# Channel attention: values from split operands, another order of the first units, and a normalisation in fours

## The chip, the cores and the metric

The kernel runs on one core of a Trainium2 chip. The metric is the device time of one execution in microseconds (us). The core has TensorE (PE in the profile, with its weight loads as PEld), VectorE (DVE), ScalarE (ACT), GpSimd (POOL) and SyncE (SP), which here issues the transfers. The engines run side by side and wait for each other through semaphores.

## The reference, cut to what matters

Four layers follow each other: a cross attention over few keys, the channel attention of this change, a transformer block with two attentions and a feed-forward part, and a recurrent block. The change is in the second one, cut here to its core:

```python
for i in range(2):
    s, e = (bounds[i], bounds[i + 1])
    h = jnp.einsum('od,bdl->bol', Wq_list[i], z1ss[:, :, s:e])
    h = h + jnp.einsum('od,bdl->bol', Wi_list[i], u1ss[:, :, s:e])
    chunks.append(h)
q, k, v = jnp.split(jnp.concatenate(chunks, axis=2), 3, axis=1)
...
score = jnp.einsum('bndi,bndj->bnij', q + r_w_bias, k) * SCALE
prob = jax.nn.softmax(score, axis=-1)
attn_vec = jnp.einsum('bnij,bndj->bndi', prob, v)
x = jnp.einsum('od,bdl->bol', Wo, attn_vec) + bo + z1ss
return (x - mean) * jax.lax.rsqrt(var + LN_EPS)
```

There are 8 batch rows of 256 channels and 512 positions, 16 heads of 64, and the mean and variance run over the channels.

## The kernel before, in words

The stage works in 64 units: 8 passes over pairs of heads, and in each pass 8 batch rows. Seven passes are a loop, the eighth is written out. The inputs of a batch row, `zu` (128 partitions, four slots, 512 columns), hold both sources.

Queries and keys are three products of split operands: a number is rounded to a short float32 form (`hi`, type fp32r) and the rest is rounded to the same form (`lo`); the sum of hi x lo, lo x hi and hi x hi stands for the full product. ScalarE rounds the inputs and the weights, GpSimd subtracts to split the inputs (`x_lo`, line 775), VectorE does so for the weights (`w_lo`, line 811). In a projection the weights are stationary and 256 columns of inputs stream, 24 products for queries and 24 for keys.

Values come out turned, positions on the partitions. There the inputs are stationary (a block of 128x128) and 128 columns of the weights `wv` stream; both are plain float32, which the trace shows as two passes a product, each with its own load (line 547).

Within unit b TensorE does, in this order: scores 0 and 1 of the next unit, the transposes of strip 2, queries of the unit after next, the transposes of strip 3, keys of the unit after next, the mix of probabilities and values, scores 2 and 3 and transposes 0 of the next unit, values of the unit after next, transposes 1 of the next unit, and the output product. The two halves of a transposed strip are copied by ScalarE (line 695) and VectorE (line 828), and a strip's transposes wait for the copies of the strip before. Maxima are VectorE's, exponentials ScalarE's, and GpSimd scales the probabilities (line 780).

The order on each engine is written out by hand: the pieces of a prologue, then `unit`. After the last unit each batch row is normalised: TensorE means by a product with a constant matrix (line 643), VectorE subtracts (line 900), ScalarE squares, TensorE takes variances (line 651), ScalarE takes the logarithm and the exponential (lines 758 and 760), GpSimd multiplies (line 802), and SyncE stores.

Of the kernel before, what the change touches and what calls it, by code (L numbers as in the profile page):

```python
# [5 lines left out]
P = 128  # L6
# [362 lines left out]
def channel_attention(nc, semaphores, z, c, w_qk, w_v, w_o, bo, q_bias, out):  # L369
# [7 lines left out]
    SCALE = DH ** -0.5  # L377
    with ExitStack() as ctx:
# [8 lines left out]
        def sem(name, per_unit=0):  # L387
# [5 lines left out]
        w_raw = sb("w_raw", [P, 2, 2 * SLOTS, P])  # L393
        w_hi, w_lo = (sb("w_" + n, [P, 2, 2 * SLOTS, P], F32R) for n in ("hi", "lo"))
        wv = sb("wv", [P, 2 * SLOTS, P])
# [20 lines left out]
        w_loaded, wv_loaded, wo_loaded, qb_loaded, bo_loaded, acc_loaded = (  # L416
            sem(n + "_loaded") for n in ("w", "wv", "wo", "qb", "bo", "acc"))
# [10 lines left out]
        means_summed, centred, squared, vars_summed, logged, rooted, normed, stored = (  # L428
            sem(n) for n in ("means_summed", "centred", "squared", "vars_summed", "logged", "rooted", "normed", "stored"))
# [28 lines left out]
        def _(sp):  # L458
            open_loop(sp, loop_sems)

            def load_w(g):
                sp.dma_start(w_raw[:, :, :, :].rearrange("p a s o -> p (a s o)"), pair_of(w_qk, g)).then_inc(w_loaded, 16)

            def load_wv(g):
                sp.dma_start(wv[:, :, :].rearrange("p s o -> p (s o)"), pair_of(w_v, g)).then_inc(wv_loaded, 16)
# [27 lines left out]
            def unit(g, b, there):  # L493
                if there(3):
                    reload_zu(g, b + 3)
                if there(BATCH):
                    if b == 0:
                        sp.wait_ge(w_split, 2 * g)
                        load_w(g)
                    if b == 1:  # L500
                        sp.wait_ge(wo_split, 1 * g)
                        load_wo(g)
                    if b == 5:
                        sp.wait_ge(q_kept, of(g, 7, 1, 0))
                        load_qb(g)
                        sp.wait_ge(v_summed, of(g, 7, 1, 0))
                        load_wv(g)

            each_pass(sp, unit)
            for b in range(BATCH):  # L510
                sp.wait_ge(normed, b + 1)
                sp.dma_start(batch_rows(out, b), acc[:, b, :, :]).then_inc(stored, 16)
# [3 lines left out]
        def _(pe):  # L516
# [12 lines left out]
            def queries(g, b):  # L529
                pe.wait_ge(x_split, of(g, b, 1, 0))  # L530
                if b % BATCH == 0:
                    pe.wait_ge(w_split, 2 * g + 1 if b else 1)
                project(0, ps_a, b).then_inc(q_summed, 1)

            def keys(g, b):
                if b % BATCH == 0:
                    pe.wait_ge(w_split, 2 * g + 2 if b else 2)
# [108 lines left out]
            def variances(b):  # L646
                pe.wait_ge(squared, b + 1)
                if b >= 2:
                    pe.wait_ge(logged, b - 1)
                for m in range(CT):  # L650
                    mm = pe.matmul(ps_s[:, b % 2, 1, :], mean_of[:, :], pr[b % 2][:, m, :], start=(m == 0), stop=(m == CT - 1))
                mm.then_inc(vars_summed, 1)
# [8 lines left out]
        def _(act):  # L661
            def round_w(part, count):
                act.wait_ge(w_loaded, 16 * count)
# [83 lines left out]
            def squares(b):  # L747
                act.wait_ge(centred, b + 1)
                if b >= 2:
                    act.wait_ge(vars_summed, b - 1)  # L750
                act.activation(pr[b % 2][:, :, :], acc[:, b, :, :], ACT.Square).then_inc(squared, 1)

            def root(b):
                act.wait_ge(vars_summed, b + 1)
                if b >= 2:
                    act.wait_ge(normed, b - 1)
                rstd = pr[2][:, b % 2, :]
                act.activation(rstd, ps_s[:, b % 2, 1, :], ACT.Ln, bias=eps[:, 0:1]).then_inc(logged, 1)
                act.wait_ge(logged, b + 1)
                act.activation(rstd, rstd, ACT.Exp, scale=-0.5).then_inc(rooted, 1)  # L760

            for b in range(BATCH + 1):
                if b < BATCH:
                    squares(b)
                if b >= 1:
                    root(b - 1)

        @block.gpsimd
        def _(pool):
# [13 lines left out]
            split_inputs(1, 0)  # L783
# [15 lines left out]
            each_pass(pool, unit)  # L799
            for b in range(BATCH):  # L800
                pool.wait_ge(rooted, b + 1)
                pool.tensor_tensor(acc[:, b, :, :], acc[:, b, :, :], pr[2][:, b % 2, :].unsqueeze(1).to_broadcast([P, CT, FEAT]),
                                   ALU.mult).then_inc(normed, 1)

        @block.vector
        def _(dve):
            dve.memset(mean_of[:, :], 1.0 / TOK).then_inc(mean_made, 1)

            def split_w(part, count):
                dve.wait_ge(w_rounded, 2 * count + part - 1)  # L810
# [38 lines left out]

            split_w(0, 1)  # L850
            split_w(1, 1)
            keep_values(1, 0)
# [3 lines left out]
            inverse(1, 0, 1)  # L856
            tops(1, 0, 2)
# [38 lines left out]
            for b in range(BATCH):  # L896
# [4 lines left out]
                ins.then_inc(centred, 1)  # L901

# [1791 lines left out]
def build(nc, semaphores, ap, out):  # L2694
# [9 lines left out]
    channel_attention(nc, semaphores, x1, ap["c"], *(ap["L1_" + n] for n in ("w_qk", "w_v", "w_o", "bo", "q_bias")), x2)  # L2704
# [16 lines left out]
def lay_out(np, a):  # L2721

    out = {}
# [32 lines left out]
    if "L1_xattn_Wo" in a:  # L2756
# [4 lines left out]
        put("L1_w_qk", w[:, :, :2].reshape(pairs, P, -1))  # L2761
        put("L1_w_v", w[:, :, 2])
# [55 lines left out]
```

## Time and profile before

| | |
|---|---|
| median of 3 runs | 4070.14 us (4067.51 to 4077.97) |
| profiled execution | 4071.54 us, its span 4069.7 us |
| mean granted TensorE clock | 0.947 |
| busy: PE, PEld | 3572.6 us (88%), 2696.4 us (66%) |
| busy: DVE, ACT, POOL | 2260.3 us (56%), 1821.8 us (45%), 1998.3 us (49%) |

The span runs from the first to the last instruction of one execution. Busy shares are averages over stages with different limits. Matmuls overlap, so a record of one is longer than the distance to the next one.

### The profile page before, as it was taken

The page shows a single profiled execution, that of the slowest core. Times are in us where ns is not written, and L with a number is a line of the kernel's source. Part 1 is how long each engine was busy: PE and PEld are TensorE (multiplying, and loading weights), DVE is VectorE, ACT ScalarE, POOL GpSimd, SP SyncE. Part 2 cuts the span into 40 slices and gives each one's busy share as a digit, 9 for nine tenths or more (in the row PEclk, how much of TensorE's full clock was granted, in tenths as well). Part 3 has the DMA queues.
Part 4 walks back from the last instruction along what each step waited for, and adds up shares of the span by engine and source line. Part 5 has one row for each costly group of instructions (what it writes and reads, how often), then busy time and mean ns, then how long its engine had stood idle before and what let it go on. Part 6 is the DMA issues. An engine that isn't in the chain of part 4 may idle for free. (4 is left out here: it accounts for less than half of the span.)

```text
span 4069.7 us, 64007 instructions
## 1 busy us (share of the span) xinstructions
PE 3572.6 (88%) x23616; PEld 2696.4 (66%) x23616; DVE 2260.3 (56%) x2778; ACT 1821.8 (45%) x4207; POOL 1998.3 (49%) x1015
## 2 busy tenths in 40 slices
PE   8969999999999999859989997699967888888876
PEld 5757676777777677547777775588845555555543
DVE  2435454444444444447777766555427777767772
ACT  1135454555555455556666665444422332323321
POOL 1145555555555555335555554355525555555552
PEclk9989999999999999989999999799979999998988
DMA  4231111111111111020021110300030000000000
GB/s 134 67 127 58 54 58 54 68 43 58 53 59 58 54 58 53 21 96 27 26 68 48 43 39 23 106 21 21 16 129 6 12 17 17 17 7 12 12 11 16
DMA packets 107558, 189.87 MB, mean 47 GB/s; under 512 B 13344, under 2 KB 32032, under 8 KB 105632
## 3 DMA queue, kind: packets, MB, share of 16 engines
q1 hardware_dynamic: 105120, 181.97, 13.1%
q8 instruction: 191, 3.13, 0.3%
q10 hardware_dynamic: 2176, 4.19, 0.3%
q14 instruction: 71, 0.58, 0.0%
HBM read 160.97 MB, written 25.17 MB: 46 GB/s over the span
## 5 line engine op out<-in xcount | busy, mean ns | idle before, releaser
L780 POOL TENSOR_TENSOR l_pr<-l_pr,l_inv 128x1024 f32<-128x1024 f32 x256 | 485.9, 1919 | 429.7 <-DVE l_inv L824 429.7
L690 ACT ACTIVATE l_pr<-l_ps_s,l_top 128x512 f32<-128x512 f32 x512 | 348.1, 691 | 385.3 <-DVE l_top L820 385.3
L1156 POOL TENSOR_TENSOR tok_pr<-tok_pr,tok_ma 128x1024 f32<-128x1024 f32 x128 | 308.0, 2407 | 309.2 <-DVE tok_pr L1530 295.2
L2288 POOL TENSOR_TENSOR rec_rs<-rec_sE,rec_rT 128x1024 f32<-128x1024 f32 x128 | 321.8, 2515 | 248.3 <-DVE rec_sE L2675 246.2
L775 POOL TENSOR_TENSOR l_x_lo<-l_zu,l_x_hi 128x2048 fp32r<-128x2048 f32 x64 | 289.5, 4523 | 274.0 <-ACT l_x_hi L674 274.0
L820 DVE TENSOR_REDUCE l_top<-l_ps_s 128x2 f32<-128x1024 f32 x256 | 301.3, 1216 | 57.8 <-PE l_ps_s L557 57.8
L565 PEld LDWEIGHTS l_ps_t<-l_ident,l_pr 128*128 128x128 f32 x2048 | 227.8, 142 | 104.5 <-issue 103.0
L2675 DVE TENSOR_TENSOR_SCAN rec_sE<-rec_wE,rec_ps_v 128x1024 f32<-128x1024 f32 x128 | 292.7, 2286 | 4.9
L557 PE MATMUL l_ps_s<-l_k,l_q 64*128 64x512 f32 x1024 | 264.6, 637 | 29.8 <-issue 29.8
L565 PE MATMUL l_ps_t<-l_ident,l_pr 128*128 128x128 f32 x2048 | 275.3, 278 | 3.6 <-ACT l_pT L695 3.6
L1400 ACT ACTIVATE tok_pr<-tok_pr,tok_shift 128x256 f32<-128x256 f32 x512 | 253.8, 499 | 27.6 <-DVE tok_shift L1538 27.3
L836 DVE TENSOR_TENSOR l_o_lo<-l_ps_a,l_o_hi 128x512 fp32r<-128x512 f32 x64 | 44.2, 691 | 381.3 <-ACT l_o_hi L700 381.3
L547 PE MATMUL l_ps_b<-l_wv,l_zu 128*128 128x128 f32 x2048 | 239.4, 275 | 0.0
L1538 DVE TENSOR_REDUCE tok_shift<-tok_pr 128x4 f32<-128x1024 f32 x128 | 155.7, 1217 | 149.6 <-POOL tok_pr L1156 147.9
L577 PE MATMUL l_ps_a<-l_pT,l_v 128*64 128x512 f32 x1024 | 235.5, 602 | 1.8 <-ACT l_pT L695 1.8
L547 PEld LDWEIGHTS l_ps_b<-l_wv,l_zu 128*128 128x128 f32 x2048 | 234.0, 192 | 0.0
L828 DVE COPY l_pT<-l_ps_t 128x512 f32<-128x512 f32 x256 | 175.4, 685 | 70.7 <-PE l_ps_t L565 70.2
L557 PEld LDWEIGHTS l_ps_s<-l_k,l_q 64*128 64x128 f32 x1024 | 91.2, 192 | 167.8 <-issue 167.3
L695 ACT ACTIVATE l_pT<-l_ps_t 128x512 f32<-128x512 f32 x256 | 152.4, 595 | 70.4 <-PE l_ps_t L565 70.4
L524 PE MATMUL l_ps_a<-l_x_hi,l_w_lo 128*128 128x256 f32 x512 | 151.7, 296 | 32.2 <-POOL l_x_lo L775 32.2
L1240 PE MATMUL tok_ps_t<-tok_ident,tok_pr 128*128 128x128 f32 x1024 | 143.1, 285 | 32.0 <-DVE tok_pT L1543 13.0
L1787 POOL TENSOR_TENSOR mlp_cube<-mlp_cube,mlp_pre 128x512 f32<-128x512 f32 x64 | 89.6, 1400 | 163.8 <-DVE mlp_cube L1950 163.8
(357 smaller groups left out, 9385.1 us busy)
## 6 DMA issues: line engine op xcount, KB each, us to landing
l_zu<-x SPq DMA_DIRECT2D x64, 512.0 KB, 3.7
l_zu<-in_c SPq DMA_DIRECT2D x64, 512.0 KB, 4.6
l_w_raw<-in_L_w_qk SPq DMA_DIRECT2D x8, 1024.0 KB, 7.6
tok_xs<-x SPq DMA_DIRECT2D x16, 512.0 KB, 3.7
x<-tok_xb SPq DMA_DIRECT2D x16, 512.0 KB, 2.8
l_xt<-in_xT SPq DMA_DIRECT2D x8, 512.0 KB, 6.5
l_ct<-in_cT SPq DMA_DIRECT2D x8, 512.0 KB, 7.8
l_xn<-in_x SPq DMA_DIRECT2D x8, 512.0 KB, 4.7
```

What stands on the lines that cost most here:

```text
L547: mm = pe.matmul(ps_b[:, t * P:(t + 1) * P], zu[b % 2][:, s, t * P:(t + 1) * P], wv[:, t // 2 * SLOTS + s, :], start=(s == 0), stop=(s == ...
L557: pe.matmul(ps_s[:, t % 2, h, :], q[b % 2][own(h), t * P:(t + 1) * P], k[b % 2][own(h), :], start=True, stop=True).then_inc(scored, 1)
L565: mm = pe.transpose(ps_t[h][:, m, :], pr[t][:, h, m * P:(m + 1) * P], ident[:, :])
L577: mm = pe.matmul(ps_a[own(h), :], v[b % 2][:, t, own(h)], pT[h][:, t, :], start=(t == 0), stop=(t == QT - 1), skip_group_check=True)
L690: act.activation(pr[t][:, h, :], ps_s[:, t % 2, h, :], ACT.Exp, bias=top[:, t, h:h + 1], accum_out=mass[:, t, h:h + 1]).then_inc(exped, 1)
L775: pool.tensor_tensor(x_lo[b % 2][:, :, :], zu[b % 2][:, :, :], x_hi[b % 2][:, :, :].bitcast(F32), ALU.subtract).then_inc(x_split, 1)
L780: pool.tensor_tensor(pr[t][:, :, :], pr[t][:, :, :], inv[:, t, :].unsqueeze(2).to_broadcast([P, 2, FEAT]), ALU.mult).then_inc(scaled, 1)
L820: dve.tensor_reduce(top[:, t, :], ps_s[:, t % 2, :, :], AXIS.X, ALU.max, negate=True).then_inc(topped, 1)
L1156: pool.tensor_tensor(tile, tile, ma[u][:, :, :].rearrange("p t k -> p (t k)").unsqueeze(1).to_broadcast([P, 2, TT * TOK]), ALU.add).then_i ...
L1400: ins = act.activation(tile, tile, ACT.Exp, bias=shift[n % RING][:, i, m:m + 1], accum_out=mass[n // 2 % 2][:, m, n % 2 * 2 + i:n % 2 * 2 ...
L2288: pool.tensor_tensor(rs[j % 2][:, :, :], sE[j % 2][:, :, :], rT[s][:, :, :], ALU.mult).then_inc(rs_made, 1)
L2675: dve.tensor_tensor_scan(sE[j % 2][:, :, :].rearrange("p c t -> p (c t)"), wE[s][:, :, :].rearrange("p c t -> p (c t)"), ps_v[j % 2][:, :, ...
```

## The change

Values become three products of split operands: the inputs' split halves, which are there for queries and keys, are stationary, and 128 columns of split weights stream. The weights of the values join `w_raw`, `w_hi` and `w_lo` as a third part; ScalarE rounds and VectorE splits them in unit 6 of each pass but the last. Each part has its own load. Inputs are loaded again after the split of two units before, without a wait for the values, and the rounding of inputs waits for the values of two units before in place of the keys.

In the prologue the first inputs are loaded ahead of the weights, the first unit's inputs are split on VectorE, the second unit's are rounded ahead of the first queries' copy, and the first two scores stand ahead of the first values.

In the normalisation GpSimd squares (into the memory of the turned probabilities `pT`), ScalarE does four logarithms and then four exponentials, twice, and the final product is GpSimd's for four batch rows and VectorE's for four.

```diff
-        w_raw = sb("w_raw", [P, 2, 2 * SLOTS, P])
...
-        wv = sb("wv", [P, 2 * SLOTS, P])
+        w_raw = sb("w_raw", [P, 3, 2 * SLOTS, P])
...
             def reload_zu(g, b):
-                sp.wait_ge(v_summed, of(g, b - 2, 1, 0))
                 sp.wait_ge(x_split, of(g, b - 2, 1, 0))
                 load_zu(b)
 
-            load_w(0)
             load_zu(0)
-            load_wv(0)
+            load_w(0, 0)
+            load_w(0, 1)
+            load_zu(1)
+            load_w(0, 2)
             load_qb(0)
-            load_zu(1)
...
                     if b == 0:
-                        sp.wait_ge(w_split, 2 * g)
-                        load_w(g)
+                        sp.wait_ge(w_split, 3 * g)
+                        for part in range(3):
+                            load_w(g, part)
...
             def values(g, b):
-                pe.wait_ge(zu_loaded[b % 2], zu_there(g, b))
                 pe.wait_ge(k_kept, of(g, b, 1, 0))
                 if b % BATCH == 0:
-                    pe.wait_ge(wv_loaded, 16 * g + 16 if b else 16)
+                    pe.wait_ge(w_split, 3 * g + 3 if b else 3)
                 for t in range(QT):
+                    here = slice(t * P, (t + 1) * P)
                     for s in range(SLOTS):
-                        mm = pe.matmul(ps_b[:, t * P:(t + 1) * P], zu[b % 2][:, s, t * P:(t + 1) * P],
-                                       wv[:, t // 2 * SLOTS + s, :], start=(s == 0), stop=(s == SLOTS - 1), skip_group_check=True)
+                        for x, w in ((x_hi, w_lo), (x_lo, w_hi), (x_hi, w_hi)):
+                            mm = pe.matmul(ps_b[:, here], x[b % 2][:, s, here], w[:, 2, t // 2 * SLOTS + s, :],
+                                           start=(s == 0 and w is w_lo), stop=(s == SLOTS - 1 and w is w_hi and x is x_hi),
+                                           skip_group_check=True)
...
             queries(1, 1)
-            values(1, 0)
             score(1, 0, 0)
             score(1, 0, 1)
+            values(1, 0)
...
             def round_inputs(g, b):
                 act.wait_ge(zu_loaded[b % 2], zu_there(g, b))
-                act.wait_ge(k_summed, of(g, b - 2, 1, 0))
+                act.wait_ge(v_summed, of(g, b - 2, 1, 0))
...
+            round_inputs(1, 0)
             round_w(0, 1)
-            round_inputs(1, 0)
             round_w(1, 1)
+            round_inputs(1, 1)
+            round_w(2, 1)
             keep_queries(1, 0)
             keep_keys(1, 0)
-            round_inputs(1, 1)
...
                 if there(1):
                     exponentials(g, b + 1, 0)
+                if b == 6 and there(BATCH):
+                    act.wait_ge(v_summed, of(g, 7, 1, 0))
+                    round_w(2, g + 1)
                 keep_turned(g, b, 2)
...
-            def squares(b):
-                act.wait_ge(centred, b + 1)
...
+            def logarithm(b):
+                act.wait_ge(vars_summed, b + 1)
+                act.activation(pr[b // 2][:, b % 2, :], ps_s[:, b % 2, 1, :], ACT.Ln, bias=eps[:, 0:1]).then_inc(logged, 1)
...
+            for first in (0, HALF):
+                for b in range(first, first + HALF):
+                    logarithm(b)
+                for b in range(first, first + HALF):
+                    root(b)
...
-            split_inputs(1, 0)
+            pool.wait_ge(x_split, of(1, 0, 1, 0))
             split_inputs(1, 1)
...
+            def squares(b):
+                pool.wait_ge(centred, b + 1)
+                if b < 2:
+                    pool.wait_ge(mixed, of(PAIRS, BATCH - 1, 2, 1))
+                else:
+                    pool.wait_ge(vars_summed, b - 1)
+                pool.tensor_tensor(pT[b % 2][:, 0:CT, :], acc[:, b, :, :], acc[:, b, :, :], ALU.mult).then_inc(squared, 1)
+
             for b in range(BATCH):
+                squares(b)
+            for b in range(HALF):
                 pool.wait_ge(rooted, b + 1)
...
+            dve.wait_ge(x_rounded, of(1, 0, 1, 0))
+            dve.tensor_tensor(x_lo[0][:, :, :], zu[0][:, :, :], x_hi[0][:, :, :].bitcast(F32), ALU.subtract).then_inc(x_split, 1)
             split_w(0, 1)
             split_w(1, 1)
-            keep_values(1, 0)
+            split_w(2, 1)
             tops(1, 0, 0)
             tops(1, 0, 1)
             inverse(1, 0, 0)
             inverse(1, 0, 1)
+            keep_values(1, 0)
...
                     tops(g, b + 1, 1)
+                if b == 6 and there(BATCH):
+                    split_w(2, g + 1)
                 keep_turned(g, b, 2)
...
+            for b in range(HALF, BATCH):
+                dve.wait_ge(rooted, b + 1)
+                dve.tensor_tensor(acc[:, b, :, :], acc[:, b, :, :], pr[b // 2][:, b % 2, :].unsqueeze(1).to_broadcast([P, CT, FEAT]),
+                                  ALU.mult).then_inc(normed[1], 1)
```

## Rows read from the trace of the kernel before

**Rows 1.** Busy time by stage (us from the start; columns as named in the head).

```profile
core 0: us, PE busy (x) PEld busy (x) DVE busy (x) ACT busy (x) POOL busy (x), PEclk, DMA share, GB/s
...
208.00:268.00 60.00, 32.47 (x213) 27.99 (x214) 17.21 (x20) 19.89 (x36) 22.19 (x11) 0.75 0.49 179
268.00:1697.00 1429.00, 1392.39 (x9389) 1025.02 (x9388) 674.52 (x1028) 720.96 (x1524) 753.65 (x313) 0.99 0.15 53
1697.00:1747.00 50.00, 30.84 (x66) 11.95 (x64) 11.47 (x18) 38.85 (x40) 18.80 (x8) 0.89 0.22 84
```

**Rows 2.** Groups of TensorE, 300 to 1600 us: busy us, mean ns | idle before.

```profile
L565 PE MATMUL l_ps_t<-l_ident,l_pr 128*128 128x128 f32 x1832 | 246.3, 278 | 0.0
L557 PE MATMUL l_ps_s<-l_k,l_q 64*128 64x512 f32 x920 | 238.8, 639 | 29.8 <-issue 29.8
```

**Rows 3.** Timeline of TensorE, two steady units (start us, us).

```profile
304.08 3.74 PE L547 MATMUL l_ps_b<-l_wv,l_zu 128*128 128x128 f32 x32
...
326.01 3.74 PE L547 MATMUL l_ps_b<-l_wv,l_zu 128*128 128x128 f32 x32
329.58 1.04 PE L565 MATMUL l_ps_t<-l_ident,l_pr 128*128 128x128 f32 x8
```

**Rows 4.** Timeline of a queries block, first and last of five products.

```profile
335.03 0.28 PE L524 MATMUL l_ps_a<-l_x_hi,l_w_hi 128*128 128x256 f32 x1
...
335.51 0.28 PE L524 MATMUL l_ps_a<-l_x_hi,l_w_lo 128*128 128x256 f32 x1
```

**Rows 5.** Timeline of the last output product, after a wait.

```profile
1695.73 0.19 PEld L592 LDWEIGHTS l_ps_a<-l_o_hi,l_wo_lo 128*128 128x128 f32 x1 [2.30 <-DVE l_o_lo L836]
1695.73 0.50 PE L592 MATMUL l_ps_a<-l_o_hi,l_wo_lo 128*128 128x512 f32 x1 [1.42 <-DVE l_o_lo L836]
1695.83 0.19 PEld L592 LDWEIGHTS l_ps_a<-l_o_lo,l_wo_hi 128*128 128x128 f32 x1
1696.07 0.40 PE L592 MATMUL l_ps_a<-l_o_lo,l_wo_hi 128*128 128x512 f32 x1
```

**Rows 6.** Groups of weight loads over the whole span.

```profile
L547 PEld LDWEIGHTS l_ps_b<-l_wv,l_zu 128*128 128x128 f32 x2048 | 234.0, 192 | 0.0
...
L577 PEld LDWEIGHTS l_ps_a<-l_pT,l_v 128*64 128x64 f32 x1024 | 68.6, 137 | 121.4 <-issue 110.6 <-ACT l_pT L695 2.3
```

**Rows 7.** Timeline of the prologue, ScalarE, VectorE and GpSimd.

```profile
215.38 1.06 ACT L664 ACTIVATE l_w_hi<-l_w_raw 128x1024 fp32r<-128x1024 f32 x1 [20.21 <-DMA l_w_raw<-in_L_w_qk]
218.09 1.91 ACT L674 ACTIVATE l_x_hi<-l_zu 128x2048 fp32r<-128x2048 f32 x1 [1.66 <-DMA l_zu<-in_c]
...
220.98 4.68 DVE L811 TENSOR_TENSOR l_w_lo<-l_w_raw,l_w_hi 128x1024 fp32r<-128x1024 f32 x1 [3.29 <-ACT l_w_hi L664]
...
234.55 4.49 POOL L775 TENSOR_TENSOR l_x_lo<-l_zu,l_x_hi 128x2048 fp32r<-128x2048 f32 x1 [9.96 <-ACT l_x_hi L674]
...
262.82 4.51 POOL L775 TENSOR_TENSOR l_x_lo<-l_zu,l_x_hi 128x2048 fp32r<-128x2048 f32 x1 [1.48 <-ACT l_x_hi L674]
```

**Rows 8.** Line 811 (duration ns min/median/max), and the timeline of a steady unit.

```profile
L811 DVE TENSOR_TENSOR l_w_lo<-l_w_raw,l_w_hi x16: 1212/1222/4685, 216.5 to 1493.9; 128x1024 fp32r<-128x1024 f32 x16
...
423.13 0.68 DVE L828 COPY l_pT<-l_ps_t 128x512 f32<-128x512 f32 x1
423.53 0.59 ACT L695 ACTIVATE l_pT<-l_ps_t 128x512 f32<-128x512 f32 x1
425.38 1.03 PE L565 MATMUL l_ps_t<-l_ident,l_pr 128*128 128x128 f32 x8
```

**Rows 9.** Timeline of the epilogue.

```profile
1706.89 1.88 PE L643 MATMUL l_ps_s<-l_acc,l_mean_of 128*128 128x512 f32 x4
1708.81 1.28 DVE L900 TENSOR_TENSOR l_acc<-l_acc,l_ps_s 128x512 f32<-128x512 f32 x2 [2.15 <-PE l_ps_s L643]
1713.03 1.28 ACT L758 ACT_TABLE_LOAD   x1
1717.91 1.28 ACT L758 ACT_TABLE_LOAD   x1
1740.52 2.34 POOL L802 TENSOR_TENSOR l_acc<-l_acc,l_pr 128x1024 f32<-128x1024 f32 x1 [1.60 <-ACT l_pr L760]
```

More of the change, by code:

```diff
@@ L391, in sem @@
             return s
-        w_raw = sb("w_raw", [P, 2, 2 * SLOTS, P])
-        w_hi, w_lo = (sb("w_" + n, [P, 2, 2 * SLOTS, P], F32R) for n in ("hi", "lo"))
-        wv = sb("wv", [P, 2 * SLOTS, P])
+        w_raw = sb("w_raw", [P, 3, 2 * SLOTS, P])
+        w_hi, w_lo = (sb("w_" + n, [P, 3, 2 * SLOTS, P], F32R) for n in ("hi", "lo"))
         wo_raw = sb("wo_raw", [P, TOK])
@@ L415, in channel_attention @@
         ident_made, mean_made, eps_made = sem("ident_made"), sem("mean_made"), sem("eps_made")
-        w_loaded, wv_loaded, wo_loaded, qb_loaded, bo_loaded, acc_loaded = (
-            sem(n + "_loaded") for n in ("w", "wv", "wo", "qb", "bo", "acc"))
+        wo_loaded, qb_loaded, bo_loaded, acc_loaded = (sem(n + "_loaded") for n in ("wo", "qb", "bo", "acc"))
+        w_loaded = [sem(f"w_loaded{part}") for part in range(3)]
         w_rounded, w_split, wo_rounded, wo_split = (sem(n) for n in ("w_rounded", "w_split", "wo_rounded", "wo_split"))
@@ L427, in channel_attention @@
         y_summed, added = sem("y_summed", CT), sem("added", CT)
-        means_summed, centred, squared, vars_summed, logged, rooted, normed, stored = (
-            sem(n) for n in ("means_summed", "centred", "squared", "vars_summed", "logged", "rooted", "normed", "stored"))
+        means_summed, centred, squared, vars_summed, logged, rooted, stored = (
+            sem(n) for n in ("means_summed", "centred", "squared", "vars_summed", "logged", "rooted", "stored"))
+        normed = [sem(f"normed{i}") for i in range(2)]
         block = ctx.enter_context(nc.Block())
@@ L459, in _, with load_w @@
             open_loop(sp, loop_sems)
[L461 to L465, printed above, removed]
+            def load_w(g, part):
+                source = w_qkv[g, :, part, :] if isinstance(g, int) else w_qkv[bass.ds(g, 1), :, part, :].rearrange("o p n -> p (o n)")
+                sp.dma_start(w_raw[:, part, :, :].rearrange("p s o -> p (s o)"), source).then_inc(w_loaded[part], 16)
             def load_wo(g):
@@ L650, in variances @@
                 for m in range(CT):
-                    mm = pe.matmul(ps_s[:, b % 2, 1, :], mean_of[:, :], pr[b % 2][:, m, :], start=(m == 0), stop=(m == CT - 1))
+                    mm = pe.matmul(ps_s[:, b % 2, 1, :], mean_of[:, :], pT[b % 2][:, m, :], start=(m == 0), stop=(m == CT - 1))
                 mm.then_inc(vars_summed, 1)
@@ L662, in round_w @@
             def round_w(part, count):
-                act.wait_ge(w_loaded, 16 * count)
+                act.wait_ge(w_loaded[part], 16 * count)
                 act.activation(w_hi[:, part, :, :], w_raw[:, part, :, :], ACT.Copy).then_inc(w_rounded, 1)
@@ L745, in _ @@
             act.wait_ge(eps_made, 1)
-            def squares(b):
-                act.wait_ge(centred, b + 1)
-                if b >= 2:
-                    act.wait_ge(vars_summed, b - 1)
-                act.activation(pr[b % 2][:, :, :], acc[:, b, :, :], ACT.Square).then_inc(squared, 1)
-            def root(b):
[L754 to L758, printed above, removed]
-                act.wait_ge(logged, b + 1)
[L760 to L766, printed above, removed]
+            def logarithm(b):
+                act.wait_ge(vars_summed, b + 1)
+                act.activation(pr[b // 2][:, b % 2, :], ps_s[:, b % 2, 1, :], ACT.Ln, bias=eps[:, 0:1]).then_inc(logged, 1)
+            def root(b):
+                act.wait_ge(logged, b + 1)
+                act.activation(pr[b // 2][:, b % 2, :], pr[b // 2][:, b % 2, :], ACT.Exp, scale=-0.5).then_inc(rooted, 1)
+            for first in (0, HALF):
[3 more added lines that the diff above has]
+                    root(b)
         @block.gpsimd
@@ L809, in split_w @@
             def split_w(part, count):
-                dve.wait_ge(w_rounded, 2 * count + part - 1)
+                dve.wait_ge(w_rounded, 3 * count + part - 2)
                 dve.tensor_tensor(w_lo[:, part, :, :], w_raw[:, part, :, :], w_hi[:, part, :, :].bitcast(F32),
@@ L2703, in build @@
     semaphores.clear()
-    channel_attention(nc, semaphores, x1, ap["c"], *(ap["L1_" + n] for n in ("w_qk", "w_v", "w_o", "bo", "q_bias")), x2)
+    channel_attention(nc, semaphores, x1, ap["c"], *(ap["L1_" + n] for n in ("w_qkv", "w_o", "bo", "q_bias")), x2)
     semaphores.clear()
```

18 lines of the change are left out of this document (8 added, 10 removed).

## The prediction

> **What bounds the kernel now.** I read the table by stages first. Of 4069.7 us of span, 1429 us are the 64 units of channel attention, and there TensorE is busy 1392 us at a granted clock of 0.99, the next engine (GpSimd) 754 [rows 1]. The groups of the steady part ask whether that busy time is a real bound: of 1300 us TensorE stands idle 29.8 us, all of it "issue" ahead of the first score of a pass, some 4.2 us at each of seven jumps back, and the transposes, the group with most instructions, wait for nothing [rows 2]. So in a unit nothing but TensorE's own order counts: a microsecond added to its instructions is a microsecond of the span, 64 times over. The unit repeats every 21.9 us, and its values take 3.57 us, from the first of 32 passes to the transposes that follow [rows 3]: 112 ns a pass. Prologue (208 to 268 us) and epilogue (1697 to 1747 us) are different: TensorE is half idle or idle, and chains over ScalarE, GpSimd and VectorE set the time [rows 1]. Each is costed by itself.
>
> **The values.** Removed: 16 full-precision products a unit, which the trace shows as 32 passes of 128 columns with a load of 128 weight columns each, 3.57 us. Added: 48 products of split operands, 128 columns streamed, again with a new stationary 128x128 block each (the stationary operand is the activations, and two neighbours never share a block). No row shows a split product of only 128 columns, so its spacing is bounded. The stream: 256 columns come every 120 ns (0.48 us for four) [rows 4], so 128 columns would take about 60 ns. That is the bound from below. The load: after a wait of 1.4 us, with nothing ahead of it, a split product's load starts at 1695.73; its product of 512 columns is shown as 0.50 us, where those behind it take 0.39 to 0.40, so it really streams from about 1695.83, 0.10 to 0.11 us after its load began. The next load starts at 1695.83, when this product streams, although the engine had stood ready since 1695.73 [rows 5]. So one load is in flight ahead of one product, not more, and it takes some 0.11 us before its product can stream. That it is filling time and no fixed delay follows from the sizes: the load's record is 192 ns for 128 columns and 137 ns for 64, 0.86 ns a column, 110 ns for 128 [rows 6]. The spacing is then the longer of stream and load, and for 128 columns the load is the longer. I take 110.5 ns: 0.108 for the load and 0.0025 until the next one starts; the full-precision passes, also one load each, keep 112. From above stands the 120 ns of the row of 256 columns. So 48 x 0.1105 = 5.30 us against 3.57: +1.73 us a unit, x 64 = **+110.7 us**. With 120 ns it is 5.76 us, +140 us; with the stream alone 2.88 us, -44 us. The number of multiplications falls from four to three, but loads rise from 32 to 48, and loads are what is paid.
>
> The Trainium skill speaks on both sides of this step. Its page "TensorE: Matmul & The Clock Gate" gives under "LDWEIGHTS (loading the stationary operand)" a load of P columns as P / 1.2 ns, 107 ns for 128, which the trace agrees with (0.10 to 0.11 us, rows 5); by it alone the values are 48 x 107 = 5.1 us. The same page's "Back-to-back issue gap" gives about 81 ns a pair at 128 columns, by which the values would be 3.9 us and this term +20 us; no run here shows that pace for 4-byte operands.
>
> **Weights of the values, rounding and splitting.** Each pass gets one more rounding on ScalarE and one more split on VectorE, in unit 6 between work that feeds transposes. The splits so far last 1.22 us alone [rows 8]. In a steady unit VectorE copies the third strip's transpose at 423.13, ScalarE at 423.53; the fourth's transposes start at 425.38 and need both [rows 8]. With the edit ScalarE rounds first (423.53 to 424.6), VectorE splits until 425.85 and copies until about 426.5. The first half of the fourth's transposes is free at 425.38, its second half would start at 425.8 and now starts at 426.5: about 0.75 us on TensorE in each of seven passes, **+5 us**. Behind VectorE queue the reciprocals of the next unit and GpSimd's scaling, which have until the end of the unit. GpSimd has nothing to run just then, as its scaling waits for those reciprocals; if it did, the split could last 4.68 us, as it did at 220.98 beside a GpSimd subtraction that ended at 224.6 [rows 7, 8], and the seven would cost +30 us. Below, with the copy's wait hidden: 0.
>
> The loads of the units now wait for the split of two units before, not also for the values; the rounding of inputs waits for those values, which ended in the unit before. Both are off TensorE's order: 0 either way, covered by the 21.9 us of a unit.
>
> **Order of the first units.** Now: weights land at 215.38, inputs at 218.09, ScalarE rounds them in 1.91 us, GpSimd splits them in 4.49 us, so that TensorE starts at about 224.6; the second unit's inputs are rounded behind the first's keys and split from 234.55 to 239.04; the third's are split from 262.82 to 267.33, and TensorE takes them up then [rows 7]. After: inputs are asked for first and land near 215.4 (the first megabyte's time now), are rounded by 217.3 and split on VectorE in about 2.4 us (twice the 1.22 us of half the size [rows 8]), then the queries' weights until 220.9: TensorE starts 3.7 us earlier. It runs queries and keys to 228.3. The second unit's inputs, landed near 221.5, are rounded by 223.4 and split by 228, so the second queries start near 228.3, not 239. From there I follow TensorE: queries 2.9, two scores 2.0, values 5.3, keys 2.9, two scores 2.0, transposes 0.9, values 5.3, transposes 0.9: 250.5. ScalarE then rounds the third inputs to 253 and GpSimd splits to 257.5. The third queries start at 257.5 instead of 267.3: 9.8 us earlier with two dear values (2 x 1.73) already in, so the order alone is worth **-13 us**. If the memory is later than the second unit's split needs, this can shrink to -4 (the first start alone).
>
> **Normalisation.** Now ScalarE sets it: each batch row has two table loads of 1.28 us, and the pattern repeats every 4.88 us [rows 9]. Fours take 16 loads down to 4 and squares go to GpSimd. ScalarE is free, but the chain passes elsewhere. A product of GpSimd on this shape lasts 2.34 us [rows 9]. TensorE does means and variances in order, each some 1.72 us (1.88 with its drain) [rows 9]; TensorE's two blocks are 3.4 us a row, but block, subtraction (1.28 [rows 9]) and square in line, every second row, make it about 3.65. The first square ends near 1702.9 (from 1697: block 1.7, subtraction 1.3, square 2.3, hand-overs 0.5), the eighth 7 x 3.65 later, near 1728. Only then does GpSimd scale the first four (9.4 us, to 1737.5), while the last logarithms and exponentials end near 1734 and VectorE scales the other four (1.2 us each). The split at 220.98 shows that VectorE with two operands in that memory stands still while GpSimd runs [rows 7], so the two add up: 1728 + 9.4 + 4.9 = 1742.4, against 1742.9 now [rows 9]. The last stores then lie closer together. I take **0**; if the two overlap, -5; if the stores queue, +3.
>
> **Sum.** 110.7 + 5 - 13 + 0 = +102.7 us. The profiled execution took 4071.54 us (span 4069.7), 1.4 over the median of the three runs, so 4071.5 + 102.7 = **4174 us**, slower by 2.5%.
>
> **Rivals.** *Loads hide behind one another* (the other side): the pace is that of the stream, 60 ns. For it: 256 columns run at 120 ns with loads under them [rows 4]. Against it: no load in rows 5 starts before the product ahead of it streams. Then -44 + 5 - 13 = -52 us, 4019. It decides below 77 ns, where 64 x (48 x 0.077 - 3.57) just pays for the other 8 us; chance 0.07. *A middle pace* of about 80 ns, loads and streams partly under each other: 64 x (3.84 - 3.57) - 8 = +9 us, 4081, about no change; against it again rows 5; chance 0.03. That is where the page's 81 ns would end. *The short stream costs double*: split products of 128 columns stream more slowly than those of 256, or the clock falls to its lower level while TensorE streams only half of the time; the spacing is 220 ns, 10.56 us a unit, +447 - 8, 4510. Against it: the transposes, with the same 128 columns and loads, pass at 110 ns, (1.04 - 0.28) / 7 for a block of eight, in a stage at clock 0.99 [rows 1 to 3]. Chance 0.05. *The loads decide, but the side terms go otherwise*: splits beside GpSimd (+25), prologue gain lost (+9), 120 ns a product (+29); each alone stays between 4174 and 4205 and belongs to the main case.
>
> **How the numbers follow.** Main case 0.85. Its own ends: 109 ns, no delay in unit 6 and overlapping scalings give 4071.5 + 106 - 13 - 5 = 4159; 120 ns and a lost start give 4071.5 + 140 + 5 - 4 = 4212. The ends rarely meet, but the transfer times are estimates, so 4145 to 4210. About 0.3% (12 us) is what a measurement can tell from no change: faster 0.07 (the loads hidden), within 0.04 (the middle pace, and 0.01 of the main case's edge), slower 0.89 (0.84 and the double cost's 0.05).
>
> **What would show it.** Right: the values' block of 48 passes lasts 5.2 to 5.4 us in a steady unit and the unit 23.6; loads start 0.11 us apart; the second queries start near 228; unit 6 is about 0.7 us longer; the epilogue still ends some 45 us after its first means. Wrong: passes 60 to 80 ns apart, or any new idle time of TensorE in the steady units, or a clock under 0.9 there.

## The result, and the profile after

The changed kernel takes 4168.53 us (median of 4 runs, 4163.83 to 4172.61), the kernel before 4071.45 us in the same comparison (4 runs, 4067.51 to 4077.97): ratio 1.0236 [1.0218, 1.0255], slower. The forecast was 4174. The profiled execution after took 4172.61 us, span 4170.8.

Stages first, as in [rows 1]: the first 49.55 us up to the third unit's queries, the units, and the normalisation, from the first memset of the stage on GpSimd to that of the next stage.

```profile
core 0: us, PE busy (x) PEld busy (x) DVE busy (x) ACT busy (x) POOL busy (x), PEclk, DMA share, GB/s
208.40:257.95 49.55, 32.99 (x241) 28.33 (x241) 20.73 (x22) 21.17 (x37) 17.19 (x10) 0.84 0.64 236
257.95:1787.73 1529.78, 1500.31 (x10385) 1132.77 (x10386) 682.84 (x1035) 727.63 (x1531) 754.54 (x313) 0.99 0.14 49
1787.73:1837.12 49.39, 28.71 (x65) 11.38 (x63) 20.04 (x22) 15.01 (x20) 25.28 (x13) 0.87 0.22 85
```

TensorE is still the engine that is busy through the units, at the same granted clock of 0.99. The whole stage goes from 1538.2 us (208.87 to 1747.06 before) to 1628.7, so +90.5. It can be taken apart by the starts of the units in the two traces:

| Part of the stage | Change, us | Forecast |
|---|---|---|
| start of the stage to the third queries (58.51 to 49.55; holds two dear values) | -9.0 | -9.8 |
| 62 further units, each 23.69 instead of 21.93 | +109.1 | +107 |
| unit 6 of seven passes: 25.16, 1.47 above the others | +10.3 | +5 |
| first unit behind each of six jumps back: its excess over an ordinary unit falls from 42.9 to 22.1 in all | -20.8 | 0 |
| first unit of the stage | +1.2 | 0 |
| normalisation (49.83 to 49.39) | -0.4 | 0 |

The parts add up to +90.4. The rest of the difference lies in later stages, whose code is the same: 797.4, 435.3 and 1090.0 us before, 805.5, 435.9 and 1092.3 after. Most of it comes with the change all the same. In the first of these stages TensorE now waits twice for nothing that the profile shows, at a place where it did not wait before, and more packets of instructions move in that stage (packets, MB, share of 16 engines; first before, then after with the two waits):

```profile
q8 instruction: 49, 0.80, 0.4%
```

```profile
2061.39 0.71 PE L1245 MATMUL tok_ps_s<-tok_kT,tok_qT 32*128 32x256 f32 x8 [3.90 <-issue]
2064.46 1.24 PE L1245 MATMUL tok_ps_s<-tok_kT,tok_qT 32*128 32x256 f32 x8 [2.35 <-issue]
```

```profile
q8 instruction: 58, 0.95, 0.5%
```

All six kernels of this study with split values have the two waits and the 58 packets; the five with full-precision values have 49 and no such waits. From GpSimd's 32nd to its 48th product on `tok_pr`, the stretch with the two waits, the first group takes 93.2 to 95.4 us and the second 88.7 to 88.8. That is 4.4 to 6.7 us of cost outside the changed stage. Why those packets move again there was not tried.

**The values**, which answer to [rows 3]. The timeline of TensorE in the same pass, with its weight loads in the first lines:

```profile
321.17 0.19 PEld L546 LDWEIGHTS l_ps_b<-l_w_lo,l_x_hi 128*128 128x128 f32 x1
321.20 0.30 PE L546 MATMUL l_ps_b<-l_w_lo,l_x_hi 128*128 128x128 f32 x1
321.28 0.19 PEld L546 LDWEIGHTS l_ps_b<-l_w_hi,l_x_lo 128*128 128x128 f32 x1
321.34 0.28 PE L546 MATMUL l_ps_b<-l_w_hi,l_x_lo 128*128 128x128 f32 x1
321.39 0.19 PEld L546 LDWEIGHTS l_ps_b<-l_w_hi,l_x_hi 128*128 128x128 f32 x1
321.46 0.27 PE L546 MATMUL l_ps_b<-l_w_hi,l_x_hi 128*128 128x128 f32 x1
...
326.59 1.06 PE L565 MATMUL l_ps_t<-l_ident,l_pr 128*128 128x128 f32 x8
...
344.89 0.30 PE L546 MATMUL l_ps_b<-l_w_lo,l_x_hi 128*128 128x128 f32 x1
```

From 321.20 to 326.59, 48 products take 5.39 us, 112.3 ns each. Each load starts 0.11 us behind the one before, about when the product ahead of it begins to stream. The next unit's values begin 23.69 us later.

**Idle time of TensorE**, which answers to [rows 2]: the groups of 300 to 1600 us (busy us, mean ns | idle before).

```profile
L546 PE MATMUL l_ps_b<-l_w_lo,l_x_hi 128*128 128x128 f32 x857 | 237.3, 277 | 0.0
...
L565 PE MATMUL l_ps_t<-l_ident,l_pr 128*128 128x128 f32 x1720 | 232.1, 277 | 7.4 <-DVE l_pT L836 4.6 <-ACT l_pT L695 2.8
L557 PE MATMUL l_ps_s<-l_k,l_q 64*128 64x512 f32 x856 | 218.8, 631 | 15.2 <-issue 15.2
```

Two things are new. The transposes wait 7.4 us, where they waited 0.0: that is unit 6. And the idle time ahead of the scores has halved, from 29.8 to 15.2 us: those are the jumps back, of which there are six (about 5 us each before, not seven of 4.2 as the prediction counted them).

**Unit 6**, timelines of VectorE, ScalarE and TensorE put in one fence:

```profile
400.84 1.22 DVE L819 TENSOR_TENSOR l_w_lo<-l_w_raw,l_w_hi 128x1024 fp32r<-128x1024 f32 x1
401.97 2.35 DVE L828 TENSOR_REDUCE l_top<-l_ps_s 128x2 f32<-128x1024 f32 x2
404.64 1.06 ACT L664 ACTIVATE l_w_hi<-l_w_raw 128x1024 fp32r<-128x1024 f32 x1
405.73 1.22 DVE L819 TENSOR_TENSOR l_w_lo<-l_w_raw,l_w_hi 128x1024 fp32r<-128x1024 f32 x1 [1.41 <-ACT l_w_hi L664]
406.33 0.63 PE L565 MATMUL l_ps_t<-l_ident,l_pr 128*128 128x128 f32 x4 [0.41 <-ACT l_pT L695]
406.87 0.68 DVE L836 COPY l_pT<-l_ps_t 128x512 f32<-128x512 f32 x1
407.61 0.66 PE L565 MATMUL l_ps_t<-l_ident,l_pr 128*128 128x128 f32 x4 [0.66 <-DVE l_pT L836]
```

In one unit VectorE splits the keys' weights (400.84), which pushes the maxima back, and then the values' weights (405.73). Both copies of a transposed strip come late: TensorE waits 0.41 us for ScalarE's and 0.66 us for VectorE's.

**A jump back**: the last output product of a pass and the first scores of the next, first before the change, then after it.

```profile
441.26 0.39 PE L592 MATMUL l_ps_b<-l_o_hi,l_wo_hi 128*128 128x512 f32 x1
446.47 1.22 PE L557 MATMUL l_ps_s<-l_k,l_q 64*128 64x512 f32 x2 [4.83 <-issue]
```

```profile
448.57 0.39 PE L592 MATMUL l_ps_b<-l_o_hi,l_wo_hi 128*128 128x512 f32 x1
451.53 1.04 PE L557 MATMUL l_ps_s<-l_k,l_q 64*128 64x512 f32 x2 [2.57 <-issue]
```

The gap is 2.57 us instead of 4.83. Before, the 1 MB of inputs was asked for at 439.41 and 439.83, 2.2 us ahead of the end of the last product at 441.65, and the 1 MB of weights behind it at 440.55; 1.8 MB of the two moved in the gap. After, the same two transfers of the loop are asked for a whole unit earlier (418.21 and 419.36), and the inputs of the next unit at 441.89, 7 us ahead of the end of the last product; no data moves in the gap.

**Start and normalisation**, which answer to [rows 7, 9]:

```profile
214.75 1.91 ACT L674 ACTIVATE l_x_hi<-l_zu 128x2048 fp32r<-128x2048 f32 x1 [20.35 <-DMA l_zu<-in_c]
216.69 2.29 DVE L859 TENSOR_TENSOR l_x_lo<-l_zu,l_x_hi 128x2048 fp32r<-128x2048 f32 x1 [8.02 <-ACT l_x_hi L674]
222.96 4.60 POOL L772 TENSOR_TENSOR l_x_lo<-l_zu,l_x_hi 128x2048 fp32r<-128x2048 f32 x1 [13.88 <-ACT l_x_hi L674]
223.79 4.86 DVE L819 TENSOR_TENSOR l_w_lo<-l_w_raw,l_w_hi 128x1024 fp32r<-128x1024 f32 x1 [2.54 <-ACT l_w_hi L664]
253.39 4.51 POOL L772 TENSOR_TENSOR l_x_lo<-l_zu,l_x_hi 128x2048 fp32r<-128x2048 f32 x1 [3.24 <-ACT l_x_hi L674]
...
1787.73 3.59 PE L643 MATMUL l_ps_s<-l_acc,l_mean_of 128*128 128x512 f32 x8
1815.59 1.89 POOL L804 TENSOR_TENSOR l_pT<-l_acc 128x1024 f32<-128x1024 f32 x1 [1.54 <-DVE l_acc L913]
1817.44 10.23 POOL L810 TENSOR_TENSOR l_acc<-l_acc,l_pr 128x1024 f32<-128x1024 f32 x4
1820.26 1.28 ACT L757 ACT_TABLE_LOAD   x1
1822.22 8.80 DVE L917 TENSOR_TENSOR l_acc<-l_acc,l_pr 128x1024 f32<-128x1024 f32 x4 [6.71 <-ACT l_pr L757]
```

The first queries start at 220.26 (224.68 before), the second at 227.71 (239.19), the third at 257.95 (267.38). In the normalisation the last square comes at 1815.59 and the scalings of GpSimd and VectorE run behind it; where the two meet they take turns.

### The profile page after: what moved, and what is told of

Same layout as the page of the kernel before. It is cut to its first block and busy times, and to the rows that moved or that the text cites. A ratio compares the mean times of both kernels' runs of the same rounds, so it can differ in the third digit from the quotient of the medians.

```text
span 4170.8 us, 65939 instructions
## 1 busy us (share of the span) xinstructions
PE 3682.7 (88%) x24640; PEld 2805.7 (67%) x24640; DVE 2283.7 (55%) x2791; ACT 1805.8 (43%) x4195; POOL 2001.2 (48%) x1018
## 5 line engine op out<-in xcount | busy, mean ns | idle before, releaser
L546 PE MATMUL l_ps_b<-l_w_lo,l_x_hi 128*128 128x128 f32 x1024 | 283.6, 277 | 0.0
L546 PE MATMUL l_ps_b<-l_w_hi,l_x_hi 128*128 128x128 f32 x1024 | 281.7, 275 | 0.0
L546 PE MATMUL l_ps_b<-l_w_hi,l_x_lo 128*128 128x128 f32 x1024 | 281.5, 275 | 0.0
L557 PE MATMUL l_ps_s<-l_k,l_q 64*128 64x512 f32 x1024 | 260.5, 628 | 15.2 <-issue 15.2
L546 PEld LDWEIGHTS l_ps_b<-l_w_lo,l_x_hi 128*128 128x128 f32 x1024 | 196.5, 192 | 0.8 <-issue 0.8
L546 PEld LDWEIGHTS l_ps_b<-l_w_hi,l_x_hi 128*128 128x128 f32 x1024 | 196.6, 192 | 0.0
L546 PEld LDWEIGHTS l_ps_b<-l_w_hi,l_x_lo 128*128 128x128 f32 x1024 | 196.6, 192 | 0.0
```

What stands on the lines that cost most here:

```text
L546: mm = pe.matmul(ps_b[:, here], x[b % 2][:, s, here], w[:, 2, t // 2 * SLOTS + s, :], start=(s == 0 and w is w_lo), stop=(s == SLOTS - 1 a ...
L557: pe.matmul(ps_s[:, t % 2, h, :], q[b % 2][own(h), t * P:(t + 1) * P], k[b % 2][own(h), :], start=True, stop=True).then_inc(scored, 1)
```

## Experiments

The theory: the loads of the split products set their pace (+112), unit 6 costs 10, the order of the first units gives 13 and the earlier reload of the inputs 18 to 21, at the jumps. The rivals: the pace comes from the stream or from the number of multiplications; the jumps' gain comes from the weights' transfer, or from something else in the change. Ratios are to the kernel before, run beside them (4070.51 us, 10 runs, for e1 to e4; 4068.84, 15 runs, for e5 to e8). "Stage" is channel attention in the profile of that run, "gaps" TensorE's idle times at the six jumps.

| Kernel | Median us (runs) | Ratio [95%] | Stage us | Gaps us |
|---|---|---|---|---|
| before | | | 1538.2 | 4.83-5.13 |
| after | 4168.53 (4) | 1.0236 [1.0218, 1.0255] | 1628.7 | 2.44-2.68 |
| e1 | 4057.14 (5) | 0.9961 [0.9948, 0.9975] | 1523.4 | 4.86-5.14 |
| e2 | 4059.59 (6) | 0.9972 [0.9958, 0.9985] | 1523.2 | 2.5-4.2 |
| e3 | 4328.23 (4) | 1.0626 [1.0608, 1.0644] | 1789.5 | 0.53-0.87 |
| e4 | 4186.65 (5) | 1.0283 [1.0269, 1.0297] | 1646.6 | 4.72-5.27 |
| e5 | 4049.82 (5) | 0.9952 [0.9939, 0.9966] | 1516.8 | 2.44-2.96 |
| e6 | 4159.92 (5) | 1.0216 [1.0202, 1.0230] | 1619.0 | 2.34-2.78 |
| e7 | 4035.19 (5) | 0.9916 [0.9902, 0.9929] | 1502.5 | 2.43-2.90 |
| e8 | 4069.75 (11) | 1.0004 [0.9995, 1.0013] | 1538.5 | 4.87-5.18 |
| e9 | 4163.27 (1; before 4064.78) | | 1620.4 | 2.40-2.70 |

**e1: the change without its values.** Full-precision values back, with the wait of the reload that belongs to them; the new order and the normalisation in fours stay.

```diff
+                sp.wait_ge(v_summed, of(g, b - 2, 1, 0))
...
-                        for x, w in ((x_hi, w_lo), (x_lo, w_hi), (x_hi, w_hi)):
-                            mm = pe.matmul(ps_b[:, here], x[b % 2][:, s, here], w[:, 2, t // 2 * SLOTS + s, :],
...
+                        mm = pe.matmul(ps_b[:, here], zu[b % 2][:, s, here], w_raw[:, 2, t // 2 * SLOTS + s, :],
+                                       start=(s == 0), stop=(s == SLOTS - 1), skip_group_check=True)
```

> The changed kernel with the full-precision values put back (32 passes a unit; inputs loaded again only after the values that read them; no rounding and splitting of a third part of the weights), new order of the first units and the normalisation in fours kept. My theory: the values cost +113 us and the split in unit 6 +10, the order of the first units gives -12, the fours 0, and the jump back of a pass gets its old idle time again (+20) because the inputs are again loaded late: about 12 us under the kernel before, 4055 to 4064. Rival, the first units' gain is lost later in the run: same time as before, 4067 to 4078. Unit 21.93 us, idle time at a jump 4.9 us by the theory, 2.5 us if that came with the new order.

The stage is 14.8 us shorter than before, the unit 21.93 us again, the gaps as long as before. So order and normalisation together are worth some -14, and everything dear in the change hangs on the values and the split of their weights. The idle time of the scores is back too:

```profile
L559 PE MATMUL l_ps_s<-l_k,l_q 64*128 64x512 f32 x912 | 236.6, 639 | 29.9 <-issue 29.9
```

**e2: two products of three.** 32 loads instead of 48, all else as after.

```diff
-                        for x, w in ((x_hi, w_lo), (x_lo, w_hi), (x_hi, w_hi)):
+                        for x, w in ((x_lo, w_hi), (x_hi, w_hi)):
```

> The changed kernel without the product of hi inputs and lo weights in the values: 32 products and 32 loads a unit in place of 48 (it leaves that third of the sum out). Theory, a load of 128 columns each 112.3 ns sets the pace: 16 fewer x 0.1123 x 64 = -115 us, 4053, values 3.6 us, unit 21.9. Rival, another engine or the copy behind the values limits the unit by now: less than half of it, above 4110.

109 us less than after, a third of 48 x 112.3 ns x 64 = 345 us being 115. An ordinary unit lasts 21.90 us in place of 23.69, 1.79 us for 16 products, 112 ns each; some 9 us were lost again at the jumps, where two gaps of this run are long (4.21 and 3.62 us). Price per product, then, and 32 split products cost about what 32 full-precision passes did.

**e3: half the stream, all the loads.**

```diff
+                        half = slice(t * P, t * P + DH)
...
-                            mm = pe.matmul(ps_b[:, here], x[b % 2][:, s, here], w[:, 2, t // 2 * SLOTS + s, :],
+                            mm = pe.matmul(ps_b[:, half], x[b % 2][:, s, here], w[:, 2, t // 2 * SLOTS + s, 0:DH],
```

> The changed kernel with only 64 of 128 columns streamed in each of the 48 products of the values (half of the values are left out); the stationary blocks and their loads stay. Theory, the load sets the pace: the spacing stays at 109 to 112 ns and the time within 15 us of 4168. Rival, the stream sets it (short split streams take two cycles a column): the spacing falls to 56 to 60 ns and the time by 48 x 0.054 x 64 = 165 us, to about 4003.

It told the two apart, and did something that neither theory gave. The timeline of TensorE inside one block of values:

```profile
333.16 0.28 PE L547 MATMUL l_ps_b<-l_w_hi,l_x_lo 128*128 128x64 f32 x1
333.27 0.28 PE L547 MATMUL l_ps_b<-l_w_hi,l_x_hi 128*128 128x64 f32 x1
333.38 0.32 PE L547 MATMUL l_ps_b<-l_w_lo,l_x_hi 128*128 128x64 f32 x1
333.52 0.40 PE L547 MATMUL l_ps_b<-l_w_hi,l_x_lo 128*128 128x64 f32 x1
333.73 0.40 PE L547 MATMUL l_ps_b<-l_w_hi,l_x_hi 128*128 128x64 f32 x1
333.94 0.40 PE L547 MATMUL l_ps_b<-l_w_lo,l_x_hi 128*128 128x64 f32 x1
```

Up to 333.38 the products start 0.11 us apart, with 64 columns as with 128: 2452 of the 3008 distances in the trace lie between 110 and 119 ns, with a mean of 111.7. The stream is not what they wait for. Then the distance is 0.21 us: 511 distances lie at 210 to 219 ns, and the clock of that stretch, which was 0.99 after the change, is down:

```profile
258.00:1787.00 1529.00, 1516.41 (x9454) 1165.99 (x9451) 619.94 (x938) 665.93 (x1398) 695.75 (x286) 0.88 0.14 48
```

So part of the time runs at the lower of the two levels (1.2 GHz instead of 2.4), where the products come at half the pace, and the kernel is 160 us slower than after.

e2 and e3 leave one rival: a fixed price of 112 ns for any product with a load of its own. No run changed the width of the load. That the columns of the load set the 112 ns is therefore read from [rows 5, 6], not shown by a run. Products as such can come closer together: in the next stage of the trace before, groups of four products with loads of 32 columns each (line 1254) start 7 ns apart, and the groups 109 ns apart.

**e4: the old wait of the reload put back.**

```diff
             def reload_zu(g, b):
+                sp.wait_ge(v_summed, of(g, b - 2, 1, 0))
                 sp.wait_ge(x_split, of(g, b - 2, 1, 0))
```

> The changed kernel with the old wait of the inputs' reload for the values of two units before, nothing else. Theory, the instructions after the jump back come late when inputs and weights are on their way at that moment: idle time ahead of the first score 2.5 -> about 4.9 us, units around the jump up by 3 us in all, six jumps: +15 to +21 us, 4184 to 4190. Rival, the shorter idle time comes from TensorE's longer program of short products: 2.5 us stays, 4168.

+17.9 us in the stage and +18.1 in the median against after, gaps as before. The removed wait, which the prediction costed at 0, is thus worth 18 us. The DMA queues in the gap that begins at 449.09, first 448.5 to 451.0, then 451.0 to 452.2 (packets, MB, share of 16 engines):

```profile
q1 hardware_dynamic: 426, 0.84, 102.4%
```

```profile
q1 hardware_dynamic: 137, 0.40, 92.8%
q8 instruction: 1, 0.02, 5.2%
```

The data queue fills the engines, and the one packet of instructions (16 KB) moves only at 451.24, 2.15 us into the gap. In the trace of before it is 443.65, 2.0 us into the gap. In the trace after, 448.71, 0.25 us ahead of it, with nothing else on the engines.

**e5: in the kernel before, the inputs' reload later instead of earlier**, behind the first scores of the next pass.

```diff
                 if there(3):
+                    if b == 0:
+                        sp.wait_ge(scored, of(g, 1, 2 * QT, 1))
                     reload_zu(g, b + 3)
```

> The kernel before with one more wait: in the first unit of a pass the reload of inputs, and the load of weights behind it, wait for the first score after the jump. Theory, the idle time at the jump is instructions that come late beside 2 MB of data: 4.9 -> 2.5 us, and less time at the lower clock after it, six jumps: -15 to -20 us, 4050 to 4056. Rival, the jump costs 4.9 us in a kernel with long products whatever the transfers do: 4071.

The jump of e5 that answers to the two above:

```profile
442.72 0.39 PE L594 MATMUL l_ps_b<-l_o_hi,l_wo_hi 128*128 128x512 f32 x1
445.56 0.70 PE L559 MATMUL l_ps_s<-l_k,l_q 64*128 64x512 f32 x2 [2.45 <-issue]
```

A wait more, and the stage is 21.4 us shorter: not the wait itself matters but whether the transfer is under way at the jump. Earlier (after) and later (e5) both help.

**e6: the third rounding and split of unit 6 one strip later.**

```diff
-                if b == 6 and there(BATCH):
-                    split_w(2, g + 1)
                 keep_turned(g, b, 2)
...
                 keep_turned(g, b, 3)
+                if b == 6 and there(BATCH):
+                    split_w(2, g + 1)
```

(ScalarE's rounding likewise, behind its copy of the keys.)

> The changed kernel with the rounding and splitting of the values' weights in unit 6 moved behind the copies of keys and of strip 3, where ScalarE and VectorE wait. Theory: the 1.47 us by which unit 6 is longer goes, seven passes: -10 us, about 4158. Rival, the split falls beside GpSimd's subtraction there and is held up with all behind it: 4168 or more.

The stage is 9.7 us shorter than after, and all units but those behind a jump last 23.69 us. The fourth strip's transposes of unit 6 stand in one block again, with no wait:

```profile
406.69 1.03 PE L565 MATMUL l_ps_t<-l_ident,l_pr 128*128 128x128 f32 x8
```

**e7: e1 with e5's wait.** The order of the first units and the fours, full-precision values, and the reload behind the jump.

> Full-precision values, the new order of the first units, the normalisation in fours, and the late reload of the first unit in a pass. If the two gains add up: 4057 - 15 to 20 = 4037 to 4042, the fastest of all; if both are the same time (the idle time at a jump is made up elsewhere): 4055.

The two gains add up (1538.2 - 14.8 - 21.4 = 1502.0; measured 1502.5). This is the fastest kernel of the study, 0.84% ahead of before.

**e8: in the kernel before, the weights' transfer alone moved away from the jump.**

```diff
                 if there(BATCH):
-                    if b == 0:
+                    if b == 2:
                         sp.wait_ge(w_split, 2 * g)
```

> The kernel before with the megabyte of queries' and keys' weights asked for two units later, inputs reloaded where they were. Theory: the inputs' megabyte is still under way at the jump, so a part of the gain of the late reload: idle time 3 to 4.5 us, -4 to -12 us, 4059 to 4067. Rival (the weights alone are in the way): all of it, 4050 to 4056.

No gain, gaps unchanged. Both guesses for it fell: the inputs' megabyte alone is enough for the long gap (0.7 to 0.8 MB moved in it).

The packet of instructions can be followed through all 66 jumps of the eleven profiles. In 65 of them the first score starts 1.68 to 1.91 us after the last such packet has ended (2.29 us in one of e2), however long the gap. Two runs move the packet without any data in the gap. In e2 it takes 2.0 and 2.1 us at two jumps, where others take 0.9 to 1.4, and these are its long gaps. In e3 it begins 1.9 to 2.4 us ahead of the gap, and the gap is 0.5 to 0.9 us. A jump of e2, the packets from 433.5 to 438.6 around its gap (two, of 2.0 us each), and a jump of e3:

```profile
438.65 2.08 PE L557 MATMUL l_ps_s<-l_k,l_q 64*128 64x512 f32 x4 [4.21 <-issue]
```

```profile
q8 instruction: 2, 0.03, 4.9%
```

```profile
473.87 1.56 PE L558 MATMUL l_ps_s<-l_k,l_q 64*128 64x512 f32 x6 [0.53 <-issue]
```

**e9: all eight last scalings on VectorE** (in the kernel after, one run).

```diff
-            for b in range(HALF):
-                pool.wait_ge(rooted, b + 1)
-                pool.tensor_tensor(acc[:, b, :, :], acc[:, b, :, :], pr[b // 2][:, b % 2, :].unsqueeze(1).to_broadcast([P, CT, FEAT]),
...
-            for b in range(HALF, BATCH):
+            for b in range(BATCH):
```

> The changed kernel with all eight final products on VectorE, none on GpSimd; the rest as it is. Theory, VectorE and GpSimd hold each other up where both have two operands in the memory: each product 1.21 to 1.22 us, the first four under the last square and the last logarithms, the last one ends some 4 us earlier after the first means, about 39.5 us in place of 43.3; of the whole time that is within its spread, 4160 to 4172. Rival, products of this form on VectorE last 2.2 us by themselves: 43 us stay.

First means to the end of the last scaling: 41.3 us (1783.32 to 1824.63), against 43.3 after (1787.73 to 1831.02). That is half of the gain hoped for. VectorE's products last 1.21 to 1.23 us alone, which rules out the rival; one lasts 2.92 beside GpSimd's last square, and that square is held up as well, by the product before:

```profile
1811.18 2.81 POOL L804 TENSOR_TENSOR l_pT<-l_acc 128x1024 f32<-128x1024 f32 x1 [1.54 <-DVE l_acc L909]
```

The two engines take turns: the square ends at 1813.98, 1.75 us after VectorE's first product (it lasts 1.89 alone), and VectorE's second ends 1.08 us after the square. The 2 us gained here can't be told from no change in one run of the whole: of the 8.3 us by which its stage is shorter than after, 5.0 lie ahead of the normalisation, where the two kernels do the same.

## Why the prediction was right, step by step

**Values: right, and for its reason.** Forecast 110.5 ns a product and 1.73 us a unit, measured 112.3 ns and 1.76 (the block of values alone takes 1.82 more, 5.39 less 3.57). The 2.5 ns that the forecast adds between loads stand in no row. What held was the reading of one load after a wait [rows 5], 0.10 to 0.11 us before its product could stream; e3 shows that the stream has no part in it at full clock, e2 that the price goes by products, and e4 less e1 gives the whole of it: 1646.6 - 1523.4 = 123.2 us for values and split, which is 64 x 1.76 = 112.6 and 10.6 for unit 6. The Trainium skill's page "TensorE: Matmul & The Clock Gate" gives P / 1.2 ns for a load of P columns under "LDWEIGHTS (loading the stationary operand)", for 128 columns an estimate of 107 ns, near the 112.3 ns a product that this trace shows. The 81 ns a pair at 128 columns that the Trainium skill gives on the same page under "Back-to-back issue gap" is not reached here by any product of 128 columns with a 128x128 block of its own: the values come 112.3 ns apart, the transposes 109 ns.

**Unit 6: right mechanism, half the size.** Forecast 0.75 us in each of seven passes, measured 1.47. The row it stood on [rows 8] was of an ordinary unit, where VectorE copies at 423.13. In unit 6 the split of the keys' weights, left over from unit 5, already holds VectorE (400.84), and the rounding delays ScalarE's copy as well, so that both halves of the transposes wait. e6 takes the 10 us away.

**Order of the first units: right.** -9.8 us forecast up to the third queries, -9.0 measured; the first start came 3.95 us earlier, counted from the start of the stage (15.81 to 11.86; 3.7 forecast). The third weights' split met a GpSimd split (4.86 us at 223.79), as such a pair did before [rows 7], but nothing waited for it.

**Normalisation: right in sum, by two errors that cancel.** The squares took 1.89 us, not 2.34, and the last scaling ended 43.3 us after the first means (45.4 forecast). That the scalings of the two engines add up held where they met: VectorE's end 1.08 us after the GpSimd product beside them (3.25 and 3.35 us with the wait, 1.21 alone), and GpSimd's fourth waited in its turn (3.33 us, 2.34 alone). But the stores, which now lie together, took until 6.1 us after the last scaling (4.2 before). In all -0.4 us.

**The step that failed** is the sentence on the loads of the units: "Both are off TensorE's order: 0 either way, covered by the 21.9 us of a unit." The cover was right for the data: no product waits for it. But at a jump back TensorE waits for something else, and a megabyte under way then makes that wait twice as long (e8: 4.9 to 5.2 us, after: 2.4 to 2.7). The prediction had the 29.8 us of "issue" in its rows and took them as given. Freeing the reload gave 18 us (e4), 20.8 by the starts of the units: 14.6 of idle time and the rest in slower products behind a long gap. The granted clock of the 10 us behind a gap was 0.68 to 0.84 before; after, it was 0.83 four times and 1.00 twice.

So the nearness of 4174 and 4168.5 owes something to luck. The stage was forecast at +102.7 and came out at +90.5: -20.8 at the jumps, +5 in unit 6 and +2 in the values. The next stage, for which the prediction has no term, put some 6.5 us back: between the medians lie 97.1 us.

**Rivals.** Loads behind one another (4019) and the middle pace (4081) fall with the 112.3 ns. The fall of the clock, priced at 220 ns a product, did not come with 128 columns (0.99). With 64 it did (e3), at 210 to 219 ns for a sixth of the products: its price was right for a product at the lower clock, its condition was not met by this change.

**Open.** That TensorE waits at a jump for the 16 KB packet, and that data ahead of it only makes the packet late, fits all 66 jumps, the long gaps of e2 and the short ones of e3 among them. It is still read from traces: no run was made to move that packet by itself. What the 1.7 to 1.9 us between the packet and the first score consist of, and whether the added waits in the next stage are of the same kind, was not tried.

## What to carry to other kernels

Where every product brings a new stationary block, count the products, each with its load, and not multiplications: fewer passes in arithmetic can be more time. Cost an insertion from the row of the very unit that it goes into, not from an ordinary one. And look at what is under way on the DMA queues when a loop jumps back: a transfer that no instruction waits for can still lengthen the jump. Compare the stages that were not touched, too: here one of them got longer in every kernel with split values.

## What the runs showed of the hardware that was not expected

- At a jump back TensorE's first product starts 1.7 to 1.9 us after a 16 KB packet of instructions has ended (65 of 66 jumps). With the data queue quiet the gap is 2.3 to 3.0 us in five kernels (after, e5, e6, e7, e9); with 0.7 to 1.9 MB of data moving in it the packet begins 1.9 to 2.5 us into the gap, which is 4.7 to 5.3 us long (before, e1, e4, e8).
- Split products of 64 and of 128 columns come 112 ns apart alike at the full clock, but the mean granted clock of the stage is 0.88 with 64 and 0.99 with 128.
- VectorE and GpSimd take turns in both directions: a GpSimd square of 1.89 us took 2.81, a GpSimd scaling of 2.34 us took 3.33, a VectorE scaling of 1.21 us took 2.92 to 3.35.
- A stage whose code is unchanged took 4.4 to 6.7 us longer in one stretch behind all six kernels with split values, with nine more packets of instructions and two waits of TensorE for nothing that the profile shows.
